# Masks on GpSimd, a later maximum, and gathers that add into the shared output

## The chip, the core and the metric

The program runs on one core of a Trainium2 chip. Its time is device microseconds, the median of three runs: 634.32 us for the kernel before (633.57 to 634.75). The five engines each work through their own queue in program order and wait for each other by semaphores: TensorE (PE; its weight loads are PEld), VectorE (DVE), ScalarE (ACT), GpSimd (POOL) and SyncE (SP), which issues most DMAs.

## The reference

`x` is 8 x 512 x 256 in f32. It is normalised, and goes two ways, a local attention of 32 heads and a mixture of 8 experts with top-1 routing, and the two results are multiplied:

```
xn = layernorm(x)
qkv = xn @ qkv_w.T                       # 32 heads of 8
attn = (q @ k.T) * 8**-0.5
attn = where(m != 0, attn * m, -inf)     # m: local window, keys i-8 .. i+7, weights that fall off
s = softmax(attn) @ v @ proj_w.T + proj_b
out = sum over experts e of where(expert_idx == e, (silu(xs @ gate_w[e]) * (xs @ up_w[e])) @ down_w[e], 0)
shared = silu(xn @ shared_gate_w) * (xn @ shared_up_w) @ shared_down_w
g = silu(out + shared)
x = x + s * g
```

## The kernel before, in words

The attention runs in 64 steps (U). A step n has 64 queries (two blocks of 32) against 47 keys each (KW), for all 32 heads: the scores fill 128 partitions x 16 groups x 47 = 752 elements. The work for a step is spread over three steps of the loop, and each engine has a loop of its own over n = 0 .. 66, written out by hand:

- TensorE, `scores(n)`: for each of the two halves of the heads a bf16 matmul with the identity brings the mask (0 or -3e38) into PSUM (L916), and two f32 matmuls add q times k (L920). It waits until the step before has been read (`a_mul`).
- VectorE, `weigh(n)` (L722): scores times the window's weights, from PSUM into `Sx`. `largest(n)` (L729): the maximum of each row, right behind it.
- GpSimd, `subtract(n)` (L427): `Sx` minus the maximum, in place.
- ScalarE, `exps(n-1)` (L500): exp, first in the step after.
- VectorE, `flipped(n-1)` (L751): two transposes into `PTs`, in the step after, behind `largest(n)`.
- TensorE, `weighted(n-2)` (L945): times v. VectorE, `invert(n-2)` (L759): reciprocals of the sums. ScalarE, `o_out(n-2)` (L470): four copies PSUM to `Or`. VectorE, `divide(n-2)` (L768) and `turned(n-2)` (L776): normalise, transpose into `OT`. TensorE then projects (`output`, L953) and VectorE adds the bias (`attention`, L794), each second step.

Beside that run the routing (steps 8 to 10, with scatters from GpSimd up to step 16), the shared expert of a batch in steps n % 8 = 0 .. 5 (gates sg at 0 and 2, su at 1 and 3, sd at 4 and 5, which ScalarE copies into the shared rows and posts with `f_sh`), the projections of q and k0 at n % 4 = 0 and of k1 at n % 4 = 1 (ScalarE copies them, `qk_out`, behind its `silu` in the step), and from step E0 = 18 to step 39 the 39 expert tiles, two a step.

The final part handles 16 pairs c of token tiles. `silu_at` puts pair c into step 41 + c for c up to 13, pairs 14 and 15 into steps 61 and 62; `result_at` is one step later, or more. `gather(c)` fetches the experts' rows of the pair into a buffer `Y` by two indirect DMAs (L439), for c = 0 .. 2 in step 40, then for pair c + 3 in the step after silu's issue point for c. `combine(c)` on GpSimd adds `Y` to the shared rows (L447). ScalarE's `silu(c)` takes the tanh of the sum into `Y` (L554), VectorE's `silu(c)` multiplies (L800), and `result(c)` does the product with the attention (L807) and the sum with x (L810), which SyncE stores.

Of the kernel before, what the change touches and what calls it, by code (L numbers as in the profile page):

```python
# [11 lines left out]
ALU = mybir.AluOpType  # L12
# [3 lines left out]
P = 128  # L16
BATCH, SEQ, C = 8, 512, 256
# [4 lines left out]
KC = C // P  # L22
# [6 lines left out]
QB = 32  # L29
# [34 lines left out]
C_M = C_ID + P  # L64
C_BIAS = C_M + KW
C_HEAD = C_BIAS + C
C_STAY = C_HEAD + HS
C_TRI, C_ONE = C_STAY, C_STAY + P
C_FIRST = C_ONE + P
C_TILE = C_FIRST + E  # L70
# [4 lines left out]
def constants(bias):  # L75

    c = np.zeros((P, C_END), np.float32)
    c[:, C_ID:C_ID + P] = np.eye(P)
    c[:, C_BIAS:C_BIAS + C] = bias
    c[:, C_HEAD:C_HEAD + HS] = np.arange(P)[:, None] // HD % HS == np.arange(HS)  # L80
    c[:, C_TRI:C_TRI + P] = np.triu(np.ones((P, P)), 1)
    c[:, C_ONE:C_ONE + P] = 1.0
    c[:, C_FIRST:C_FIRST + E] = E - np.arange(E)
    c[:, C_TILE:C_TILE + NT] = np.arange(NT)
    at = np.arange(KW)[None, :] - (np.arange(P) % QB)[:, None]
    band = (at >= 0) & (at < 2 * WIN)
    d = np.abs(at - WIN).astype(np.float32)
    c[:, C_M:C_M + KW] = np.where(band, (WIN - d / 2.0) / WIN * np.float32(HD ** -0.5), 1.0)
    key = np.arange(KW)[None, :]
    kinds = (band & (key >= WIN), band, band, band, band, band & (key < QB + WIN))  # L90
    c[:, C_MASK:] = np.concatenate([np.where(k, 0.0, NEG) for k in kinds], 1)
    return c


# [3 lines left out]

def mask_kind(n):
    return 0 if n % UB == 0 else 2 if n % UB == UB - 1 else 1  # L100


def first_key(n):
# [48 lines left out]
def build(nc, x, wqkv_d, wproj_d, router_w, gate_w, up_w, down_w, sgate_w, sup_w, sdown_w,  # L152
# [3 lines left out]
    with ctx:  # L156
# [3 lines left out]
        def sem(name):  # L160
            return ctx.enter_context(nc.semaphore(name))
# [52 lines left out]
        XR = [EB[:, (3 + i) * CT * C:(4 + i) * CT * C] for i in range(3)]  # L214

        ident = cst[:, C_ID:C_ID + P]
        mw = cst[:, C_M:C_M + KW]
        bias = cst[:, C_BIAS:C_BIAS + C]
        tri = rcst[:, C_TRI - C_STAY:C_TRI - C_STAY + P]
# [7 lines left out]
        def shared_rows(t):  # L227
# [10 lines left out]
            sem("r_" + n) for n in ("sc", "tanh", "sce", "oh", "cnt", "slot", "row", "tab"))  # L238
        r_scat = [sem(f"r_scat{i}") for i in range(SENDS)]
        m_full = [sem(f"m_full{i}") for i in range(MB)]  # L240
        a_qk, a_S, a_mul, a_max, a_sub, a_exp, a_PT, a_V, a_PV, a_O, a_rec, a_nrm, a_OT, a_s = (
            sem("a_" + n) for n in ("qk", "S", "mul", "max", "sub", "exp", "PT", "V", "PV", "O", "rec", "nrm", "OT", "s"))
        x_v, x_vd = ([sem(f"x_{n}{i}") for i in range(2)] for n in ("v", "vd"))
        f_tg, f_ag, f_hT, f_sh = (sem("f_" + n) for n in ("tg", "ag", "hT", "sh"))
        b_in, b_wd, b_st = ([sem(f"b_{n}{i}") for i in range(k)] for n, k in (("in", 4), ("wd", 2), ("st", 3)))
        b_wg = [sem(f"b_wg{i}") for i in range(2)]
        b_xT, b_et, b_ea, b_hT, b_y = (sem("b_" + n) for n in ("xT", "et", "ea", "hT", "y"))
        d_y, d_x, d_st = ([sem(f"d_{n}{i}") for i in range(3)] for n in ("y", "x", "st"))
        d_z, d_t, d_w, d_g, d_o = (sem("d_" + n) for n in ("z", "t", "w", "g", "o"))

        x_tiles = x.rearrange("(t p) c -> p t c", p=P)
        out_v = out.rearrange("(t p) c -> p t c", p=P)
# [150 lines left out]
        def _(pool):  # L403
# [15 lines left out]
            def scatter(t):  # L419
                pool.wait_ge(r_row, t + 1)  # L420
                pool.indirect_dma_start(xs_dram, bass.IndirectOffsetOnAxis(ap=slot[:, t:t + 1], axis=0),
                                        X[:, t, :], None).then_inc(r_scat[t // (T // SENDS)], 16)

            def subtract(n):
                pool.wait_ge(a_max, n + 1)
                s = Sx[n % 3][:, :, 0:KW]
                nc.gpsimd.tensor_tensor(s, s, mx[n % 3][:, :].unsqueeze(2).broadcast_to([P, 2 * G, KW]),  # L427
                                        ALU.subtract).then_inc(a_sub, 1)

            def gather(c):  # L430
                b = c % 3
                if c == 0:
                    for k in range(3):
                        pool.wait_ge(b_st[k], 16 * len(range(k, NX, 3)))
                if c >= 3:
                    pool.wait_ge(d_w, c - 2)
                for k in range(CT):
                    t = c * CT + k
                    pool.indirect_dma_start(Y[b][:, k * C:(k + 1) * C], None, ys_dram,  # L439
                                            bass.IndirectOffsetOnAxis(ap=slot[:, t:t + 1], axis=0)).then_inc(d_y[b], 16)  # L440

            def combine(c):
                b = c % 3
                z = shared_rows(c * CT).rearrange("p t c -> p (t c)")
                pool.wait_ge(d_y[b], 16 * CT * (c // 3 + 1))
                pool.wait_ge(f_sh, c + 1)
                nc.gpsimd.tensor_tensor(z, Y[b], z, ALU.add).then_inc(d_z, 1)  # L447

            for n in range(LAST + 1):
                for c in silu_at(n):  # L450
                    combine(c)
                if n < U:
                    subtract(n)
                if n == SENT:
                    pool.wait_ge(s_fill, 16 * 10)
                    pool.wait_ge(r_slot, 1)
                for t in range((n - SENT) * SPS, min((n - SENT + 1) * SPS, T)):
                    if t >= 0:
                        scatter(t)
                if n == C_STEP:  # L460
                    for c in range(3):
                        gather(c)
                for c in silu_at(n - 1):
                    if c + 3 < NC:
                        gather(c + 3)

        @block.scalar
        def _(act):
# [80 lines left out]
                act.dma_start(ys_dram[i * P:(i + 1) * P, :], yb[:, i % 3, :]).then_inc(b_st[i % 3], 16)  # L549

            def silu(c):
                act.wait_ge(d_z, c + 1)
                z = shared_rows(c * CT).rearrange("p t c -> p (t c)")
                nc.scalar.activation(Y[c % 3], z, ACT.Tanh, scale=0.5).then_inc(d_t, 1)  # L554

# [60 lines left out]
        def _(dve):  # L616
# [106 lines left out]
                   mw.unsqueeze(1).unsqueeze(1).broadcast_to([P, 2, G, KW]), ALU.mult).then_inc(a_mul, 1)  # L723

            def largest(n):
                dve.wait_ge(a_mul, n + 1)
                if n >= 3:
                    dve.wait_ge(a_sub, n - 2)
                reduce(mx[n % 3][:, :], Sx[n % 3][:, :, 0:KW], AX, ALU.max).then_inc(a_max, 1)  # L729
# [94 lines left out]
            for n in range(LAST + 1):  # L824
                if n < U:
                    weigh(n)
                    largest(n)
                if n == 0:
                    variance(1)
                    deviation(1)  # L830
# [9 lines left out]
                    table()  # L840
                if 0 <= n - 1 < U:
                    flipped(n - 1)
                for i in pair_at(n, 1)[:1]:
                    gate(i)
                    gated(i)
# [8 lines left out]
                if 0 <= n - 2 < U:  # L854
                    divide(n - 2)
                    turned(n - 2)
                for c in silu_at(n):
                    silu(c)
                if n < BATCH:
# [10 lines left out]
        def _(pe):  # L870
# [34 lines left out]

            def scores(n):
                h, u = divmod(n, UH)
                if n == 0:
                    pe.wait_ge(s_cast, 2)
                if n >= 1:  # L910
                    pe.wait_ge(a_mul, n)
                if u == 0:
                    pe.wait_ge(a_qk, 3 * h + 3)
                kind = 2 * mask_kind(n)
                for j in range(KC):
                    mm(psS[:, j, 0:BW], identb[:, :], maskb[:, kind:kind + 2, :, :].rearrange("p i r k -> p (i r k)"),  # L916
                       start=True, stop=False)
                    for i in range(2):
                        k = block_of(n, i) % (HALF // QB)
                        last = mm(psS[:, j, i * HS * KW:(i + 1) * HS * KW], qBD[h % 2][:, j, k, :, :].rearrange("p s q -> p (s q)"),  # L920
                                  kBD[h % 2][:, j, :, k * QB:k * QB + KW], start=False, stop=i == 1)
                last.then_inc(a_S, 1)

            def values(t):
# [160 lines left out]
```

## Time and profile before

| | |
|---|---|
| median of 3 runs | 634.32 us |
| profiled execution | 633.25 us |
| its span in the profile | 631.4 us |
| PE busy | 557.1 us (88%) |
| DVE busy | 403.7 us (64%) |
| ACT busy | 307.9 us (49%) |
| POOL busy | 187.0 us (30%) |
| rate of all DMAs in the first of 40 slices | 292 GB/s |

The span is the profiled execution from its first to its last instruction; the rest of its time lies outside. Busy shares are means over stages with different limits, so they say little of one edit. The stages are told apart by the windows below, and a single step is read in the timeline: an instruction's start, its length, and in brackets how long its engine was idle before it and who ended that.

### The profile page before, as it was taken

What the parts mean: (1) busy time and instruction counts of PE and PEld (TensorE: products, weight loads), DVE (VectorE), ACT (ScalarE), POOL (GpSimd) and SP (SyncE); (2) the same over time, 40 slices, a digit from 0 to 9 for tenths busy, and PEclk for the clock granted to TensorE, in tenths of its full rate; (3) what the DMA queues carried; (4) which work ended last, traced back from release to release, by engine and by line L of the source; (5) the groups of instructions that cost most, each with busy time, mean ns of one, the idle gap of its engine ahead of it and who ended that gap; (6) DMA issues with size and microseconds to landing.
All of it is one profiled execution on the core that took longest, in us unless ns stands there. A gap on an engine that the chain in (4) does not pass through costs nothing. (4 is left out here: it accounts for less than half of the span.)

```text
span 631.4 us, 10599 instructions
## 1 busy us (share of the span) xinstructions
PE 557.1 (88%) x3358; PEld 479.0 (76%) x3358; DVE 403.7 (64%) x853; ACT 307.9 (49%) x762; POOL 187.0 (30%) x160
## 2 busy tenths in 40 slices
PE   1979999979889999999999999999886877769865
PEld 1757898758768999888999888898675655657754
DVE  6766556885756446456446456446688888886873
ACT  1473654458673644533634533645454533636331
POOL 6001011148861111000111000114655545532230
PEclk9989999979999999999999999999989899999997
DMA  8525441113327576576577566443133333331110
GB/s 292 180 70 174 151 141 55 49 49 99 113 92 216 163 223 202 167 203 199 143 218 208 168 203 190 126 129 115 50 110 110 108 99 101 117 102 26 35 42 17
DMA packets 107371, 82.89 MB, mean 131 GB/s; under 512 B 42293, under 2 KB 104757, under 8 KB 107317
## 3 DMA queue, kind: packets, MB, share of 16 engines
q1 hardware_dynamic: 98628, 68.72, 36.9%
q0 software_dynamic: 3072, 8.39, 4.2%
q10 hardware_dynamic: 5616, 5.11, 2.3%
q8 instruction: 27, 0.44, 0.3%
q14 instruction: 28, 0.22, 0.1%
HBM read 59.12 MB, written 23.07 MB: 130 GB/s over the span
## 5 line engine op out<-in xcount | busy, mean ns | idle before, releaser
L427 POOL TENSOR_TENSOR Sx<-Sx,mx 128x752 f32<-128x752 f32 x64 | 93.7, 1465 | 407.1 <-DVE mx L729 406.5
L945 PE MATMUL psV<-VB,PTs 128*128 128x132 f32 x1024 | 133.1, 282 | 30.2 <-ACT Or L470 29.7
L945 PEld LDWEIGHTS psV<-VB,PTs 128*128 128x128 f32 x1024 | 127.1, 193 | 36.1 <-issue 34.9
L470 ACT ACTIVATE Or<-psV 32x128 f32<-32x128 f32 x256 | 68.5, 268 | 150.5 <-DVE rs L759 146.2
L920 PE MATMUL psS<-kBD,qBD 128*128 128x188 f32 x512 | 104.0, 327 | 0.0
L920 PEld LDWEIGHTS psS<-kBD,qBD 128*128 128x128 f32 x512 | 86.9, 193 | 10.4 <-issue 2.2
L751 DVE STREAM_TRANSPOSE PTs<-Sx 128x512 f32<-128x512 f32 x128 | 82.9, 685 | 1.0 <-ACT Sx L500 1.0
L995 PE MATMUL psM<-xT,EB 128*128 128x128 f32 x624 | 76.4, 276 | 0.0
L995 PEld LDWEIGHTS psM<-xT,EB 128*128 128x128 f32 x624 | 73.8, 192 | 2.1 <-ACT qBD L489 1.3
L722 DVE TENSOR_TENSOR Sx<-psS,cst 128x752 f32<-128x752 f32 x64 | 59.6, 932 | 24.5 <-PE psS L920 24.5
L736 DVE SCALAR_TENSOR_TENSOR ea<-et,psM 128x256 f32<-128x256 f32 x39 | 16.4, 421 | 76.3 <-PE psM L995 47.2
L972 PE MATMUL psM<-xnT,wsgu 128*128 128x512 f32 x128 | 61.6, 604 | 2.1 <-DVE ag L783 2.1
L729 DVE TENSOR_REDUCE mx<-Sx 128x16 f32<-128x752 f32 x64 | 59.9, 936 | 2.2
L916 PE MATMUL psS<-maskb,identb 128*128 128x376 bf16 x128 | 41.7, 325 | 17.2 <-DVE Sx L722 16.9
L470 ACT ACTIVATE kBD<-psM 32x272 f32<-32x272 f32 x128 | 49.2, 385 | 14.7 <-PE psM L902 13.6
L500 ACT ACTIVATE Sx<-Sx 128x752 f32<-128x752 f32 x64 | 53.0, 828 | 4.9 <-POOL Sx L427 4.4
L489 ACT ACTIVATE qBD<-psM,cst 128x512 f32<-128x512 f32 x64 | 38.7, 687 | 21.3 <-PE psM L897 21.2
L768 DVE TENSOR_TENSOR O<-Or,rs 128x128 f32<-128x128 f32 x64 | 23.5, 368 | 39.9 <-issue 39.4
L1004 PE MATMUL psM<-EB,ehT 128*128 128x256 f32 x156 | 36.9, 379 | 0.0
L953 PE MATMUL psM<-wp,OT 128*128 128x256 f32 x128 | 33.6, 386 | 3.7 <-DVE OT L776 2.3
L972 PEld LDWEIGHTS psM<-xnT,wsgu 128*128 128x128 f32 x128 | 22.3, 192 | 18.1 <-issue 15.8
L902 PE MATMUL psM<-xnT,wqkv 128*128 128x272 f32 x128 | 34.8, 396 | 0.0
(107 smaller groups left out, 689.3 us busy)
## 6 DMA issues: line engine op xcount, KB each, us to landing
EB<-in_L_ffn_gate_w SPq DMA_DIRECT2D x39, 256.0 KB, 2.9
EB<-in_L_ffn_up_w SPq DMA_DIRECT2D x39, 256.0 KB, 3.6
EB<-in_L_ffn_down_w SPq DMA_DIRECT2D x39, 256.0 KB, 3.1
VB<-v_dram SPq DMA_DIRECT2D x256, 32.0 KB
stage<-xs_dram SPq DMA_DIRECT2D x39, 128.0 KB, 2.2
ys_dram<-yb ACTq DMA_DIRECT2D x39, 128.0 KB, 3.1
xs_dram<-blank SPq DMA_DIRECT2D x9, 512.0 KB, 3.8
v_dram<-vS SPq DMA_DIRECT2D x8, 512.0 KB, 2.9
```

The costliest lines, as they stand in the source:

```text
L427: nc.gpsimd.tensor_tensor(s, s, mx[n % 3][:, :].unsqueeze(2).broadcast_to([P, 2 * G, KW]), ALU.subtract).then_inc(a_sub, 1)
L470: return nc.scalar.activation(dst, src, ACT.Copy)
L489: last = nc.scalar.activation(qBD[h % 2][:, :, :, i, :], q, ACT.Copy, scale=cst[:, C_HEAD + i:C_HEAD + i + 1])
L500: nc.scalar.activation(s, s, ACT.Exp).then_inc(a_exp, 1)
L722: tt(s, psS[:, :, 0:BW].rearrange("p j (g k) -> p j g k", k=KW), mw.unsqueeze(1).unsqueeze(1).broadcast_to([P, 2, G, KW]), ALU.mult).then_ ...
L729: reduce(mx[n % 3][:, :], Sx[n % 3][:, :, 0:KW], AX, ALU.max).then_inc(a_max, 1)
L751: last = nc.vector.transpose(PTs[n % 2][:, k, :, :, :].rearrange("p j i (r q) -> p (j i r) q", q=QB), Sx[n % 3][:, :, k * QB:(k + 1) * QB])
L916: mm(psS[:, j, 0:BW], identb[:, :], maskb[:, kind:kind + 2, :, :].rearrange("p i r k -> p (i r k)"), start=True, stop=False)
L920: last = mm(psS[:, j, i * HS * KW:(i + 1) * HS * KW], qBD[h % 2][:, j, k, :, :].rearrange("p s q -> p (s q)"), kBD[h % 2][:, j, :, k * QB: ...
L945: last = mm(psV[:, j, at:at + HS * VW], PTs[n % 2][:, k, j, i, :], VB[n % 2][:, i, k, :, VW * j:VW * j + VW], start=k == 0, stop=k == 1)
L972: last = mm(ps[:, :], wsgu[:, kc, at:at + P], xnT[:, b, kc, WIN:WIN + SEQ], start=kc == 0, stop=kc == KC - 1)
L995: last = mm(ps[:, f * P:(f + 1) * P], egu[:, i % 2, kc, f * P:(f + 1) * P], xT[:, i % 2, kc, :], start=kc == 0, stop=kc == KC - 1)
```

## The change

Three things change.

1. In steps 0 to 7 and from 18 on (`masked_late`) TensorE issues no mask matmuls. GpSimd adds the mask in `banded(n)`, from a table in f32 in the constants, to what `weigh(n)` wrote. In steps 8 to 17 all stays as it was.
2. In those steps VectorE's `largest(n)` waits for the addition (`a_add`). It stands behind `flipped(n-1)` in steps 0 to 7 and 18 to 37, and behind `turned(n-2)` from step 38 (E0 + NP) on.
3. `gather(c)` adds its rows straight into the shared rows (`compute_op=ALU.add`) and `combine` is gone. The gather for the pair whose tanh is in step n+1 is issued in step n, behind `subtract(n)`, once the shared rows are there (`f_sh`). ScalarE's `silu(c)` waits for the DMA itself (`d_y`).

```diff
+def masked_late(n):
+    return n < BATCH or n >= E0

+            def banded(n):
+                pool.wait_ge(a_mul, n + 1)
+                s = Sx[n % 3][:, :, :].rearrange("p (m r) k -> p m r k", r=HS)[:, :, :, 0:KW]
+                kind = 2 * KC * mask_kind(n)
+                nc.gpsimd.tensor_tensor(s, s, band[:, kind:kind + 2 * KC, :].unsqueeze(2).broadcast_to([P, 2 * KC, HS, KW]),
+                                        ALU.add).then_inc(a_add, 1)
...
             def gather(c):
-                b = c % 3
                 if c == 0:
                     for k in range(3):
                         pool.wait_ge(b_st[k], 16 * len(range(k, NX, 3)))
-                if c >= 3:
-                    pool.wait_ge(d_w, c - 2)
+                pool.wait_ge(f_sh, c + 1)
                 for k in range(CT):
                     t = c * CT + k
-                    pool.indirect_dma_start(Y[b][:, k * C:(k + 1) * C], None, ys_dram,
-                                            bass.IndirectOffsetOnAxis(ap=slot[:, t:t + 1], axis=0)).then_inc(d_y[b], 16)
-
-            def combine(c):
-                b = c % 3
-                z = shared_rows(c * CT).rearrange("p t c -> p (t c)")
-                pool.wait_ge(d_y[b], 16 * CT * (c // 3 + 1))
-                pool.wait_ge(f_sh, c + 1)
-                nc.gpsimd.tensor_tensor(z, Y[b], z, ALU.add).then_inc(d_z, 1)
+                    pool.indirect_dma_start(shared_rows(c * CT)[:, k, :], None, ys_dram,
+                                            bass.IndirectOffsetOnAxis(ap=slot[:, t:t + 1], axis=0),
+                                            compute_op=ALU.add).then_inc(d_y[c % 3], 16)
 
             for n in range(LAST + 1):
-                for c in silu_at(n):
-                    combine(c)
                 if n < U:
+                    if masked_late(n):
+                        banded(n)
                     subtract(n)
...
-                if n == C_STEP:
-                    for c in range(3):
-                        gather(c)
-                for c in silu_at(n - 1):
-                    if c + 3 < NC:
-                        gather(c + 3)
+                for c in silu_at(n + 1):
+                    gather(c)
...
             def silu(c):
-                act.wait_ge(d_z, c + 1)
+                act.wait_ge(d_y[c % 3], 16 * CT * (c // 3 + 1))
+                if c >= 3:
+                    act.wait_ge(d_w, c - 2)
...
             for n in range(LAST + 1):
                 if n < U:
                     weigh(n)
-                    largest(n)
+                    if not masked_late(n):
+                        largest(n)
...
                 if 0 <= n - 1 < U:
                     flipped(n - 1)
+                if n < U and masked_late(n) and n < E0 + NP:
+                    largest(n)
...
                 if 0 <= n - 2 < U:
                     divide(n - 2)
                     turned(n - 2)
+                if E0 + NP <= n < U:
+                    largest(n)
...
                 for j in range(KC):
-                    mm(psS[:, j, 0:BW], identb[:, :], maskb[:, kind:kind + 2, :, :].rearrange("p i r k -> p (i r k)"),
-                       start=True, stop=False)
+                    if not late:
+                        mm(psS[:, j, 0:BW], identb[:, :], maskb[:, kind:kind + 2, :, :].rearrange("p i r k -> p (i r k)"),
+                           start=True, stop=False)
```

VectorE in a step of the final part (step 45), before; `Sx` holds the scores, `mx` the maxima, `PTs` their transposes, `O` and `OT` the output, `xnT` the shared rows, `EB` the buffers of the final part:

```order
L722 TENSOR_TENSOR Sx<-psS,cst 128x16x47
L729 TENSOR_REDUCE mx<-Sx 128x16
L751 STREAM_TRANSPOSE PTs<-Sx 128x512 x2
L759 RECIPROCAL rs<-psV 128x8 x2
L768 TENSOR_TENSOR O<-Or,rs 128x128
L776 STREAM_TRANSPOSE OT<-O 128x4x32
L800 SCALAR_TENSOR_TENSOR xnT<-EB,xnT 128x512
L807 SCALAR_TENSOR_TENSOR X<-xnT,X 128x512
L810 TENSOR_TENSOR EB<-X,EB 128x512
```

The same step on VectorE now:

```order
L726 TENSOR_TENSOR Sx<-psS,cst 128x16x47
L758 STREAM_TRANSPOSE PTs<-Sx 128x512 x2
L766 RECIPROCAL rs<-psV 128x8 x2
L775 TENSOR_TENSOR O<-Or,rs 128x128
L783 STREAM_TRANSPOSE OT<-O 128x4x32
L736 TENSOR_REDUCE mx<-Sx 128x16
L807 SCALAR_TENSOR_TENSOR xnT<-EB,xnT 128x512
L814 SCALAR_TENSOR_TENSOR X<-xnT,X 128x512
L817 TENSOR_TENSOR EB<-X,EB 128x512
```

The maximum has moved from the second place to the place behind the turned output, ahead of the silu.

GpSimd before, from the addition for pair 3 through steps 44 and 45 (gathers of pairs 5 and 6):

```order
L447 TENSOR_TENSOR xnT<-EB,xnT 128x512 [waits f_sh,d_y0]
L427 TENSOR_TENSOR Sx<-Sx,mx 128x16x47 [waits a_max]
L439 DMA EB<-ys_dram,slot 128x256 [waits d_w]
L439 DMA EB<-ys_dram,slot 128x256
L447 TENSOR_TENSOR xnT<-EB,xnT 128x512 [waits f_sh,d_y1]
L427 TENSOR_TENSOR Sx<-Sx,mx 128x16x47 [waits a_max]
L439 DMA EB<-ys_dram,slot 128x256 [waits d_w]
L439 DMA EB<-ys_dram,slot 128x256
```

GpSimd now, steps 44 and 45 (gathers of pairs 4 and 5):

```order
L435 TENSOR_TENSOR Sx<-Sx,cst 128x16x47 [waits a_mul]
L441 TENSOR_TENSOR Sx<-Sx,mx 128x16x47 [waits a_max]
L451 DMA xnT<-ys_dram,slot 128x256 [waits f_sh]
L451 DMA xnT<-ys_dram,slot 128x256
L435 TENSOR_TENSOR Sx<-Sx,cst 128x16x47 [waits a_mul]
L441 TENSOR_TENSOR Sx<-Sx,mx 128x16x47 [waits a_max]
L451 DMA xnT<-ys_dram,slot 128x256 [waits f_sh]
L451 DMA xnT<-ys_dram,slot 128x256
```

The addition of the pair has left the queue, the mask's addition has come in ahead of the subtraction, and the gathers of a step are those that the next step's tanh waits for.

ScalarE now, step 45 (k1 is copied in this step); before, the rows stood in the same order, and the tanh waited for `d_z`:

```order
L502 ACTIVATE Sx<-Sx 128x16x47 [waits a_sub]
L558 ACTIVATE EB<-xnT 128x512 [waits d_w,d_y1]
L472 ACTIVATE kBD<-psM 32x272 [waits a_S,m_full0]
L472 ACTIVATE kBD<-psM 32x272 x3
L472 ACTIVATE Or<-psV 32x128 [waits a_nrm,a_rec]
L472 ACTIVATE Or<-psV 32x128 x3
L472 ACTIVATE xnT<-psM 128x512 [waits m_full1]
```

The copies of k and then those of `Or` stand behind the tanh.

## Rows read from the trace of the kernel before

**Rows 1.** Windows by stage: PE, PEld, DVE, ACT, POOL busy us; PEclk, DMA, GB/s

```profile
27.50:111.60 84.10, 78.44 (x423) 64.88 (x423) 54.51 (x116) 43.68 (x104) 12.19 (x8) 0.98 0.37 122
...
188.20:407.00 218.80, 218.49 (x1473) 196.62 (x1472) 113.47 (x245) 103.29 (x270) 27.52 (x19) 1.00 0.64 190
...
432.00:570.00 138.00, 108.88 (x606) 89.03 (x605) 110.58 (x191) 67.72 (x158) 73.09 (x63) 0.98 0.36 102
```

**Rows 2.** Timeline of light step 55: start us, length us, engine, line, operation

```profile
561.47 0.93 DVE L722 TENSOR_TENSOR Sx<-psS,cst 128x752 f32<-128x752 f32 x1
...
562.44 0.94 DVE L729 TENSOR_REDUCE mx<-Sx 128x16 f32<-128x752 f32 x1
...
563.29 1.29 DVE L751 STREAM_TRANSPOSE PTs<-Sx 128x512 f32<-128x512 f32 x2
...
563.46 1.45 POOL L427 TENSOR_TENSOR Sx<-Sx,mx 128x752 f32<-128x752 f32 x1 [3.75 <-DVE mx L729]
...
564.78 1.11 ACT L470 ACTIVATE Or<-psV 32x128 f32<-32x128 f32 x4 [5.61 <-DVE rs L759]
...
565.98 0.29 DVE L768 TENSOR_TENSOR O<-Or,rs 128x128 f32<-128x128 f32 x1 [1.23 <-issue]
...
566.54 0.90 DVE L722 TENSOR_TENSOR Sx<-psS,cst 128x752 f32<-128x752 f32 x1
```

**Rows 3.** Timeline of VectorE: the weighing of steps 39, 47, 48, 49 and 63

```profile
427.14 0.94 DVE L722 TENSOR_TENSOR Sx<-psS,cst 128x752 f32<-128x752 f32 x1
...
492.25 0.94 DVE L722 TENSOR_TENSOR Sx<-psS,cst 128x752 f32<-128x752 f32 x1
...
500.62 0.93 DVE L722 TENSOR_TENSOR Sx<-psS,cst 128x752 f32<-128x752 f32 x1
...
510.51 0.93 DVE L722 TENSOR_TENSOR Sx<-psS,cst 128x752 f32<-128x752 f32 x1
...
611.33 0.93 DVE L722 TENSOR_TENSOR Sx<-psS,cst 128x752 f32<-128x752 f32 x1
```

**Rows 4.** Timeline near the end: the exp of step 63 and its flip

```profile
615.78 0.83 ACT L500 ACTIVATE Sx<-Sx 128x752 f32<-128x752 f32 x1
...
616.64 1.30 DVE L751 STREAM_TRANSPOSE PTs<-Sx 128x512 f32<-128x512 f32 x2 [0.16 <-ACT Sx L500]
```

**Rows 5.** Timeline of TensorE: a mask matmul and its follower

```profile
563.26 0.32 PE L916 MATMUL psS<-maskb,identb 128*128 128x376 bf16 x1
...
563.42 0.80 PE L920 MATMUL psS<-kBD,qBD 128*128 128x188 f32 x4
```

**Rows 6.** Timeline of VectorE and GpSimd at the silu of pair 14

```profile
603.20 0.65 DVE L800 SCALAR_TENSOR_TENSOR xnT<-EB,xnT 128x512 f32<-128x512 f32 x1
603.31 1.68 POOL L447 TENSOR_TENSOR xnT<-EB,xnT 128x512 f32<-128x512 f32 x1 [1.75 <-ACT xnT L470]
```

**Rows 7.** Timeline of ScalarE: copies of q and k0 (step 40)

```profile
433.16 2.42 ACT L489 ACTIVATE qBD<-psM,cst 128x512 f32<-128x512 f32 x4 [0.74 <-PE psM L897]
...
435.46 1.57 ACT L470 ACTIVATE kBD<-psM 32x272 f32<-32x272 f32 x4
```

**Rows 8.** Timeline of GpSimd: the last two gathers, each for one tile

```profile
557.48 0.97 POOL L439 DMA_INDIRECT EB<-ys_dram,slot  x1
558.76 0.95 POOL L439 DMA_INDIRECT EB<-ys_dram,slot  x1 [0.32 <-issue]
```

**Rows 9.** Windows, POOL alone: a stretch in which only the gather moves data

```profile
560.40:561.20 0.80, 0.00 (x0) 1.00 0.59 164
```

**Rows 10.** Timeline of step 45: result's product, GpSimd's addition, tanh

```profile
481.15 2.01 DVE L807 SCALAR_TENSOR_TENSOR X<-xnT,X 128x512 f32<-128x512 f32 x1
481.32 1.28 POOL L447 TENSOR_TENSOR xnT<-EB,xnT 128x512 f32<-128x512 f32 x1
482.63 0.63 ACT L554 ACTIVATE EB<-xnT 128x512 f32<-128x512 f32 x1 [1.36 <-POOL xnT L447]
```

**Rows 11.** Groups by line: busy us, mean ns, idle before, of result's product

```profile
L807 DVE SCALAR_TENSOR_TENSOR X<-xnT,X 128x512 f32<-128x512 f32 x14 | 19.0, 1360 | 0.1
```

More of the change, by code:

```diff
@@ L66 @@
 C_HEAD = C_BIAS + C
-C_STAY = C_HEAD + HS
+C_BAND = C_HEAD + HS
+C_STAY = C_BAND + 12 * KW
 C_TRI, C_ONE = C_STAY, C_STAY + P
@@ L91, in constants @@
     c[:, C_MASK:] = np.concatenate([np.where(k, 0.0, NEG) for k in kinds], 1)
+    c[:, C_BAND:C_STAY] = np.tile(c[:, C_MASK:].reshape(P, 3, 1, 2 * KW), (1, 1, KC, 1)).reshape(P, 12 * KW)
     return c
@@ L216, in build @@
         ident = cst[:, C_ID:C_ID + P]
+        band = cst[:, C_BAND:C_BAND + 12 * KW].rearrange("p (m k) -> p m k", k=KW)
         mw = cst[:, C_M:C_M + KW]
@@ L240, in build @@
         m_full = [sem(f"m_full{i}") for i in range(MB)]
-        a_qk, a_S, a_mul, a_max, a_sub, a_exp, a_PT, a_V, a_PV, a_O, a_rec, a_nrm, a_OT, a_s = (
-            sem("a_" + n) for n in ("qk", "S", "mul", "max", "sub", "exp", "PT", "V", "PV", "O", "rec", "nrm", "OT", "s"))
+        a_qk, a_S, a_mul, a_add, a_max, a_sub, a_exp, a_PT, a_V, a_PV, a_O, a_rec, a_nrm, a_OT, a_s = (
+            sem("a_" + n) for n in ("qk", "S", "mul", "add", "max", "sub", "exp", "PT", "V", "PV", "O", "rec", "nrm", "OT", "s"))
         x_v, x_vd = ([sem(f"x_{n}{i}") for i in range(2)] for n in ("v", "vd"))
@@ L248, in build @@
         d_y, d_x, d_st = ([sem(f"d_{n}{i}") for i in range(3)] for n in ("y", "x", "st"))
-        d_z, d_t, d_w, d_g, d_o = (sem("d_" + n) for n in ("z", "t", "w", "g", "o"))
+        d_t, d_w, d_g, d_o = (sem("d_" + n) for n in ("t", "w", "g", "o"))
         x_tiles = x.rearrange("(t p) c -> p t c", p=P)
@@ L725, in largest @@
             def largest(n):
-                dve.wait_ge(a_mul, n + 1)
+                if masked_late(n):
+                    dve.wait_ge(a_add, len([k for k in range(n + 1) if masked_late(k)]))
+                else:
+                    dve.wait_ge(a_mul, n + 1)
                 if n >= 3:
@@ L907, in scores @@
                 h, u = divmod(n, UH)
-                if n == 0:
+                late = masked_late(n)
+                if n == BATCH:
                     pe.wait_ge(s_cast, 2)
@@ L920, in scores @@
                         last = mm(psS[:, j, i * HS * KW:(i + 1) * HS * KW], qBD[h % 2][:, j, k, :, :].rearrange("p s q -> p (s q)"),
-                                  kBD[h % 2][:, j, :, k * QB:k * QB + KW], start=False, stop=i == 1)
+                                  kBD[h % 2][:, j, :, k * QB:k * QB + KW], start=late, stop=late or i == 1)
                 last.then_inc(a_S, 1)
```

## The prediction

> **What bounds the kernel now.** I read the busy time by stage first, then the timeline of single steps, then the waits. One step handles 64 queries of all heads; W(n) is the moment VectorE starts to weigh the scores of step n, M(n) the end of its maximum. Three stages matter. In steps 0 to 7 and above all 18 to 37 (the stage with the experts) TensorE is full: 218.49 of 218.80 us, in steps 0 to 7 78.44 of 84.10 [rows 1]. From step 39 on it has slack (108.88 of 138.00), and VectorE is at 110.58 of 138.00 [rows 1]. The steps there show no slack on VectorE's own chain. A light step lasts 566.54 - 561.47 = 5.07 us and is this chain: weigh, maximum, transposes (flip), reciprocals, ScalarE's four copies Or, product O, turned output, next weigh [rows 2]. A step with the final part (silu, result) lasts 500.62 - 492.25 = 8.37, and with a shared gate (sg) in it 510.51 - 500.62 = 9.89, so 1.5 more: ScalarE's tanh and VectorE's product stand between Or and O [rows 3].
>
> In before, the softmax of a step has nearly a step to spare: the maximum of step n ends right behind W(n), GpSimd's subtraction takes 1.45, ScalarE's exp 0.83 [rows 2, 4], and only the flip in step n+1 wants the result. The gathers have more than a step to spare as well, since they are issued two or three steps ahead.
>
> **Part 1, the mask matmuls.** Each starts 0.16 us before its follower [rows 5] (the 0.32 beside it overlaps). Two a step, in 54 of 64 steps: 17.3 us of TensorE's stream. It is worth its price only where TensorE is the bound: 20 steps x 0.32 = 6.4, and of the 8 early steps (2.6) some 1.6, since TensorE waits there now and then. **-8.0**. In the late stage it is worth nothing: VectorE's chain covers it.
>
> **Part 2, the mask on GpSimd.** No such addition is in the trace. The subtraction of the same 752 elements takes 1.45 [rows 2], the addition of 512 elements with both inputs dense 1.28 [rows 6], so 1.9 for 752. The bounds are 1.45 and 1.9. In steps below 38 the maximum stands behind the flip, which ends 1.2 us after it starts, so VectorE waits 0.3 to 0.8 us and the gate of an expert comes up that much later; the trace has about that much idle there before the gate. Hidden, **0**. From 38 on it ends long before the maximum. Beside the addition VectorE does flip and reciprocals, each with one input at most in SBUF. Loading the wider constants (564 columns more, 289 KB) delays the start by about 1 us at the 292 GB/s of the first slice; in step 0 the maximum (0.94) no longer stands ahead of the variance, which ScalarE's next work waits for: **0**.
>
> **Part 3, the maximum behind the turned output (steps 38 to 63).** The number of instructions on VectorE's chain is the same, but now M(n) lies right before W(n+1), and the flip of step n+1 needs this step's subtraction and exp. The loop from M to M: handover and subtraction 0.08 + 1.45, exp with handovers 0.9, so the flip starts at M + 2.4; flip to Or 1.49, Or to O 1.20, O to the next instruction 0.56, maximum 0.94 [rows 2, 4]. Sum 6.6, against 5.07. The wait is 1.45 in a light step. On ScalarE the copies of q and k stand between exp and Or: 433.16 to 437.03, 3.9 for q and k0 (n divisible by 4), 1.6 for k1 (the step after) [rows 7]. So:
> Step 39: 6.6. Step 40 (q, k0, sg): 2.4 + 3.9 + 1.2 + 1.5 + 0.56 + 0.94 = 10.5. Step 56 the same. Step 57: 2.4 + 1.6 + 1.2 + 1.5 (product, turned, maximum) = 6.7. Step 58: 6.6 + 1.5 = 8.1. Step 60: 6.6.
> Where VectorE has the result's two products behind the maximum (steps after 54, 58 and 62), its own work is the longer way: the product ends 0.56 behind the subtraction that holds it up [rows 10], at M + 2.1 (2.5 where a silu comes first, Part 4), the sum takes 0.7, weighing 1.0, flip to maximum 4.2. That gives 8.0 (59) and 8.4 (55, 63).
>
> **Part 4, the gathers.** Before, the gather of pair c+3 was issued in the step of pair c, GpSimd added it, and ScalarE's tanh found it ready. Now the gather for step n+1 stands behind step n's subtraction, which stands behind M(n), and the tanh of step n+1 waits for its landing. Behind the tanh on ScalarE wait the copies of q and k, and Or; for Or wait O, the turned output and M(n+1). That closes a second loop, once a step: 0.08 + 1.45, then 0.4 (VectorE's silu has both inputs in SBUF and was at work 0.11 before the GpSimd addition which took 1.68 in place of 1.28 [rows 6]), 0.14 to the gather, 3.65 from the first issue to the last byte (557.48, the second at 558.76, bytes until about 561.15 [rows 8, 9]), tanh 0.6 [rows 10], Or to O 1.20, 0.56, 0.94: 9.0, and 8.6 where no silu precedes. Add what the trace has no row for: the last byte to the waiting engine, and the cost of adding on the way. Call it a. The nearest row is the gather itself, a = 0; the upper end is twice the work on GpSimd (2.2) and twice the burst of data (0.8 us [rows 9]), 3.0. I take 0.8, the burst once more. (The Trainium skill, "DMA: Bandwidth & Descriptors", Rules for kernel authors, says that an accumulating DMA reads its destination and writes it later. No run shows it yet; it speaks for a burst twice as long rather than for 0.)
> What goes: GpSimd's additions. They held up the result's product, 2.01, where the silu of the same size takes 0.65 [rows 6, 10]. But the subtraction now lies at just that place, right behind the maximum and beside silu and result. VectorE's own way stays at 8.4 to 8.6, and the gather's loop is above it.
> Steps 41 to 54: 8.6 + 1.6 (k1) = 10.2 for 41; 13 x 9.0 = 117.0; q and k0 in 44, 48, 52 and k1 in 45, 49, 53: 16.5; sg in 42, 48, 50: 4.5. Sum 148.2 + 14a. In before they are 14 x 8.37 + 3 x 1.5 = 121.7 [rows 3]. Steps 61 and 62: 8.6 + 9.0 + 2a.
>
> **The sum.** M(38) comes where W(39) was, less part 1, with 0.3 for the wait: 427.14 - 8.0 + 0.3 = 419.4 [rows 3]. Steps 39 and 40: 17.1. Steps 41 to 54: 148.2. Step 55: 8.4. Steps 56 to 60: 10.5 + 6.7 + 8.1 + 8.0 + 6.6 = 39.9. Steps 61 to 63: 26.0. The tail was 631.4 - 611.33 = 20.1 from W(63) [rows 3]; 1.9 of it lies before M(63), and the chain of step 61 is done by then, some 2.7: 15.5. Together 674.5, with 16a = 12.8: span 687.3. The profiled execution is 1.85 above its span, and the median 1.07 above that execution: **690 us**, 56 slower. By parts: -8 from TensorE, the rest of the way, +64, from the two loops.
>
> **Rivals.**
> (A) The gather isn't waited for: the addition lands early enough or ScalarE's other work covers it, and only the softmax loop costs. Steps 41 to 54 stay at some 123, steps 55 to 63 at 71: 419.4 + 17.1 + 123 + 71 + 15.5 + 2.9 = 649. For it: in before the tanh waits little. Against: from the gather's issue to the tanh ScalarE has only the exp to do, 0.9 of 3.65.
> (B) Faster. Flip and Or do not wait, because VectorE reaches the maximum early: with GpSimd's additions gone, the results' products are back at some 0.65 (mean 1.36 [rows 11], 14 of them, 9.9 us), and -8.0 comes on top: 634.3 - 17.9 = 616. The point that decides is M(n) to M(n+1): below 8.4 in the final steps and below 5.1 in light ones. Against: 2.4 us of subtraction and exp do not fit in the 1.0 that weighing leaves.
> (C) Both loops, and a price above mine. Either a is 2 or more (16 x 1.2 = 19 on top, 709), or the port is held differently. On that, the row first: the result's product is recorded from 481.15, 0.17 before GpSimd's addition, and still ended 0.56 after it [rows 10], so GpSimd got in between. If VectorE kept its place over both products, the subtraction would end 0.9 later in 14 steps: +12, 702. The Trainium skill ("SBUF — State Buffer", Who interferes with whom) has it that whichever of the two starts first keeps the shared pair for its instruction; the 1.68 of rows 6 agrees, the recorded starts of rows 10 do not, unless the product had not really begun.
>
> **How the numbers follow.** Forecast 0.66, A 0.11, B 0.10, C 0.13. The forecast's own range, a from 0 to 2 or so: 677 to 708. The range reaches down to A and up into C: 646 to 712. A difference under 0.2% (1.3 us) can't be told from none. Faster 0.10, same 0.01, slower 0.89.
>
> **What would show it.** Right: in the profile after, ScalarE's tanh (L558) waits 2 us and more for the gathers in steps 41 to 54; steps with q and k0 last about 13.5, those without 9.5 to 10; the flip (L758) waits for exp in light steps, which last 6.6; the expert stage is about 6 us shorter; result's product is still near 2 us in many steps. Wrong: a period of 8.4 in the final steps (A), or light steps of 5.1 (B). The forecast falls if the tanh is found waiting for nothing, or if M(n) isn't followed by the gather on GpSimd.

## The result, and the profile after

The changed kernel takes 718.11 us (715.9 to 719.29, four runs), the kernel before 634.27 in the same comparison: a ratio of 1.1324, 95% interval 1.1299 to 1.1349. It is 84 us slower. The forecast was 690 us, range 646 to 712: the direction and the two loops were right, and the size was not.

The windows by stage of the profile after (columns as in [rows 1]):

```profile
190.00:404.00 214.00, 212.89 (x1440) 193.65 (x1439) 112.82 (x242) 104.28 (x272) 58.37 (x39) 1.00 0.66 192
...
430.00:600.00 170.00, 101.81 (x440) 80.92 (x439) 83.59 (x147) 53.43 (x125) 82.67 (x49) 0.79 0.28 59
600.00:717.00 117.00, 77.65 (x356) 65.81 (x354) 63.52 (x125) 35.76 (x89) 49.13 (x31) 0.76 0.19 42
```

The expert stage is still TensorE's, and a few us shorter. Behind 430 us no engine is busy for more than 60% of the time up to 600: TensorE 101.81 of 170, where [rows 1] has 108.88 of 138. Where no engine is near full, the length of a step is set by who waits for whom. From the waits of the whole execution after (who waited for whom; us in total, times, longest):

```profile
POOL Sx L441 <- DVE mx L736: 205.6, 59, 10.1
...
DVE O L775 <- issue: 104.5, 33, 9.1
ACT Sx L502 <- POOL Sx L441: 94.5, 29, 4.2
...
ACT EB L558 <- DMA xnT<-ys_dram,slot: 81.8, 14, 6.2
```

Two of them are new and are the two loops: exp (L502) waits for the subtraction, 94.5 us against 4.4 before, and the tanh (L558) for the gathers. The product O (L775) follows from them: it stands behind ScalarE's copies `Or`, which stand behind the tanh, though the profile puts its 104.5 us down to "issue". One period of the gather's loop, from the maximum of step 45 to that of step 46, in the timeline after (the rows that answer to [rows 8, 10]):

```profile
502.11 0.89 DVE L736 TENSOR_REDUCE mx<-Sx 128x16 f32<-128x752 f32 x1
502.93 0.68 DVE L807 SCALAR_TENSOR_TENSOR xnT<-EB,xnT 128x512 f32<-128x512 f32 x1
503.09 1.82 POOL L441 TENSOR_TENSOR Sx<-Sx,mx 128x752 f32<-128x752 f32 x1 [6.70 <-DVE mx L736]
503.52 1.94 DVE L814 SCALAR_TENSOR_TENSOR X<-xnT,X 128x512 f32<-128x512 f32 x1
...
505.06 1.82 POOL L451 DMA_INDIRECT xnT<-ys_dram,slot  x1 [0.15 <-issue]
...
507.19 1.55 POOL L451 DMA_INDIRECT xnT<-ys_dram,slot  x1 [0.30 <-issue]
...
511.73 0.63 ACT L558 ACTIVATE EB<-xnT 128x512 f32<-128x512 f32 x1 [5.96 <-DMA xnT<-ys_dram,slot]
512.27 1.09 ACT L472 ACTIVATE Or<-psV 32x128 f32<-32x128 f32 x4
513.45 0.29 DVE L775 TENSOR_TENSOR O<-Or,rs 128x128 f32<-128x128 f32 x1 [4.96 <-issue]
...
514.08 0.89 DVE L736 TENSOR_REDUCE mx<-Sx 128x16 f32<-128x752 f32 x1
```

Read it in order: maximum until 503.00, subtraction from 503.09, first gather 505.06, second 507.19, tanh 511.73, Or, O, next maximum until 514.97: 11.97 us, against 8.37 before. From the first issue to the tanh it is 6.67 us, where the forecast had 3.65 + 0.8 = 4.45. The subtraction takes 1.82 beside VectorE's silu and 1.45 in the light step below (the forecast had 1.45 + 0.4; this delay by an operation of the other engine is called the lock from here on), and result's product is held up to 1.94, just as GpSimd's addition had done it in [rows 10].

A light step after (step 57; answers to [rows 2]):

```profile
643.05 1.45 POOL L441 TENSOR_TENSOR Sx<-Sx,mx 128x752 f32<-128x752 f32 x1 [7.19 <-DVE mx L736]
...
644.53 0.83 ACT L502 ACTIVATE Sx<-Sx 128x752 f32<-128x752 f32 x1 [3.78 <-POOL Sx L441]
...
645.39 1.31 DVE L758 STREAM_TRANSPOSE PTs<-Sx 128x512 f32<-128x512 f32 x2 [1.25 <-ACT Sx L502]
...
648.65 0.89 DVE L736 TENSOR_REDUCE mx<-Sx 128x16 f32<-128x752 f32 x1
```

The flip waits 1.25 us for exp, and from maximum to maximum it is 6.58 (642.96 to 649.54), where 6.7 was forecast.

### The profile page after: what moved, and what is told of

It is laid out like the page before. It is cut to its first block and busy times, and to the rows that moved or that the text cites. A ratio compares the mean times of both kernels' runs of the same rounds, so it can differ in the third digit from the quotient of the medians.

```text
span 717.5 us, 10418 instructions
## 1 busy us (share of the span) xinstructions
PE 580.2 (81%) x3250; PEld 498.4 (69%) x3250; DVE 401.9 (56%) x853; ACT 308.2 (43%) x762; POOL 283.8 (40%) x198
## 3 DMA queue, kind: packets, MB, share of 16 engines
q0 software_dynamic: 6144, 8.39, 6.1%
## 5 line engine op out<-in xcount | busy, mean ns | idle before, releaser
L959 PE MATMUL psV<-VB,PTs 128*128 128x132 f32 x1024 | 157.9, 316 | 76.8 <-ACT Or L472 76.8
L959 PEld LDWEIGHTS psV<-VB,PTs 128*128 128x128 f32 x1024 | 149.1, 224 | 86.8 <-issue 86.2
L441 POOL TENSOR_TENSOR Sx<-Sx,mx 128x752 f32<-128x752 f32 x64 | 99.1, 1549 | 205.7 <-DVE mx L736 205.6
L435 POOL TENSOR_TENSOR Sx<-Sx,cst 128x752 f32<-128x752 f32 x54 | 99.3, 1838 | 196.7 <-DVE Sx L726 196.7
L934 PE MATMUL psS<-kBD,qBD 128*128 128x188 f32 x512 | 97.3, 331 | 15.0 <-DVE Sx L726 14.8
L502 ACT ACTIVATE Sx<-Sx 128x752 f32<-128x752 f32 x64 | 53.2, 831 | 94.6 <-POOL Sx L441 94.5
L775 DVE TENSOR_TENSOR O<-Or,rs 128x128 f32<-128x128 f32 x64 | 18.5, 288 | 105.0 <-issue 104.5
L736 DVE TENSOR_REDUCE mx<-Sx 128x16 f32<-128x752 f32 x64 | 58.5, 914 | 12.1 <-POOL Sx L435 11.8
L914 PE MATMUL psM<-xnT,wqkv 128*128 128x272 f32 x128 | 39.1, 434 | 18.7 <-ACT qBD L491 18.6
L451 POOL DMA_INDIRECT xnT<-ys_dram,slot x28 | 46.6, 1665 | 6.4 <-issue 5.9
L558 ACT ACTIVATE EB<-xnT 128x512 f32<-128x512 f32 x14 | 8.8, 629 | 81.8 <-DMA xnT<-ys_dram,slot 81.8
L914 PEld LDWEIGHTS psM<-xnT,wqkv 128*128 128x128 f32 x128 | 26.0, 210 | 24.6 <-ACT qBD L491 20.1
```

The source lines that it names most:

```text
L435: nc.gpsimd.tensor_tensor(s, s, band[:, kind:kind + 2 * KC, :].unsqueeze(2).broadcast_to([P, 2 * KC, HS, KW]), ALU.add).then_inc(a_add, 1)
L502: nc.scalar.activation(s, s, ACT.Exp).then_inc(a_exp, 1)
L914: last = mm(ps[:, 0:KH], wqkv[:, kc, C + j * P:C + (j + 1) * P], xnT[:, b, kc, at:at + KH], start=kc == 0, stop=kc == KC - 1)
L959: last = mm(psV[:, j, at:at + HS * VW], PTs[n % 2][:, k, j, i, :], VB[n % 2][:, i, k, :, VW * j:VW * j + VW], start=k == 0, stop=k == 1)
```

## The experiments

All ratios are to runs of the kernel before on the same chip. "Final steps" are those with silu and result; steps whose shared gate or whose copies of q and k make them longer are named apart. M(n) and W(n) are as in the prediction. The diffs are shortened: "..." and comments in them are not in the kernels, and declarations are left out.

### e1: the old gathers in the changed kernel

```diff
-                for c in silu_at(n + 1):
-                    gather(c)
+                if n == C_STEP: ... gather(0), gather(1), gather(2)
+                for c in silu_at(n - 1): ... gather(c + 3)      # into Y; combine(c) adds on GpSimd, as before
```

> The changed kernel with the gathers, their issue points and GpSimd's addition as they were before; masks on GpSimd and the late maximum stay. Theory T1 (two loops from maximum to maximum, of which the gather's is the dearer): the final steps fall from 12.0 to about 8.4 to 9.7 us, light steps stay at 6.6, ScalarE's tanh waits little; 645 to 662 us. Rival T2 (TensorE at half its clock and the softmax loop explain the time, the tanh's wait is only where it shows): still above 690.

Measured: 674.21 us, ratio 1.0644 (1.0614 to 1.0674). 44 less than the changed kernel, so T2's number fell, but T1's was 12 too low. The timeline of e1, step 47 to 48, shows why:

```profile
512.84 1.24 POOL L453 DMA_INDIRECT EB<-ys_dram,slot  x1 [0.15 <-issue]
...
514.38 0.95 POOL L453 DMA_INDIRECT EB<-ys_dram,slot  x1 [0.30 <-issue]
...
515.35 1.29 POOL L461 TENSOR_TENSOR xnT<-EB,xnT 128x512 f32<-128x512 f32 x1
...
516.67 0.63 ACT L570 ACTIVATE EB<-xnT 128x512 f32<-128x512 f32 x1 [3.11 <-POOL xnT L461]
```

Its data had landed long before, but GpSimd's addition for the next tanh stands in GpSimd's queue behind this step's subtraction and two issues (the next step's tanh is the one at 516.67). With the late maximum the tanh waits for that queue: final steps of 9.1 us, and 13.1 with q and k0. This is the nearest kernel to rival A of the prediction that keeps the buffers, and 25 us above its number (649): A had let the tanh go free because it had been free before, and here it waits for GpSimd's addition.

### e2: the same gathers, without adding

```diff
                     pool.indirect_dma_start(shared_rows(c * CT)[:, k, :], None, ys_dram,
-                                            bass.IndirectOffsetOnAxis(ap=slot[:, t:t + 1], axis=0),
-                                            compute_op=ALU.add).then_inc(d_y[c % 3], 16)
+                                            bass.IndirectOffsetOnAxis(ap=slot[:, t:t + 1], axis=0)).then_inc(d_y[c % 3], 16)
```

> The changed kernel, with gathers at the same place in GpSimd's queue that copy into the shared rows and don't add (the experts' rows replace the shared expert's). T1 with the addition as the price that was mis-sized (a = 3.0, of which the plain gather has 0.3): GpSimd's issue falls from 1.6 to 1.8 to about 1.0 us each, first issue to tanh from 6.7 to 4.0, final steps from 12.0 to 9.3; 16 x 2.7 = 43 less, 675 us (668 to 683). Rival T3 (a is the price of waiting for any gather, of the completion or of HBM behind the expert's store, not of adding): 710 or more.

This kernel leaves the addition out.

Measured: 688.72 us, ratio 1.0864 (1.084 to 1.0888). 29.4 less than with the addition, over 16 pairs 1.8 each; a plain final step takes 9.95 to 10.0 in place of 12.0. From its timeline:

```profile
505.44 1.24 POOL L451 DMA_INDIRECT xnT<-ys_dram,slot  x1 [0.15 <-issue]
...
506.99 0.95 POOL L451 DMA_INDIRECT xnT<-ys_dram,slot  x1 [0.30 <-issue]
...
510.03 0.63 ACT L557 ACTIVATE EB<-xnT 128x512 f32<-128x512 f32 x1 [3.88 <-DMA xnT<-ys_dram,slot]
```

First issue to tanh 4.59, of which 1.55 to the second issue and 3.04 from there to the tanh. Adding makes the two pieces 2.13 and 4.54. So of the 3.0 us of "a" in such a step 2.1 go with the addition (0.6 for GpSimd's longer issues, 1.5 for the way from the second issue to the tanh), and 0.9 a plain gather has as well.

About half of that 0.9 is no price of the gather. In 12 of the 16 pairs, here and in the changed kernel, the first issue runs beside VectorE's result, and there it is longer: 1.24 us against 0.97 plain (in e1 too, where no tanh waits for it), 1.82 against 1.55 adding. The other four pairs (0, 1, 14, 15) show the gather by itself. First issue to tanh is 4.0, 4.1, 4.5 and 4.0 us plain, and 5.6, 5.8, 5.6 and 5.6 adding. For pair 15 the windows (as in [rows 9]) show the bytes of the second gather, about 131 KB each time; first before, then the issue, the burst and the tanh in the changed kernel:

```profile
560.40:561.00 0.60, 0.00 (x0) 1.00 0.78 219
...
686.23 1.55 POOL L451 DMA_INDIRECT xnT<-ys_dram,slot  x1 [0.30 <-issue]
...
688.40:689.60 1.20, 1.05 (x1) 1.00 0.82 109
...
689.95 0.63 ACT L558 ACTIVATE EB<-xnT 128x512 f32<-128x512 f32 x1 [4.86 <-DMA xnT<-ys_dram,slot]
```

The burst begins 1.6 us behind the start of its issue before (558.76) and 2.2 now, which is the longer issue, and lasts 1.2 us in place of 0.6. The tanh follows some 0.4 behind it (in e2, pair 15, 0.5). These windows can be read to 0.2 us. So in a quiet stretch, with nothing beside the gather, adding costs two issues longer by some 0.55 each and a burst longer by 0.6; with 0.4 for the completion that is some 2 us over the way to the last byte before, and a plain gather has about 0.5 of it. Both theories were off in the time: most of the cost is the addition, and the rest is in part the completion, in part what goes on beside the gather.

### e3: each gather one step earlier where it can be

```diff
-                for c in silu_at(n + 1):
-                    gather(c)
+                for c in range(NC):
+                    if n == gather_at(c):    # silu's step - 2, or - 1 where f_sh comes only then
+                        gather(c)
```

> The changed kernel, with each gather issued one step earlier where the shared rows are already there (pairs 1 to 11), the rest in place. T1: the loop through the gather is open in steps 42 to 52, the tanh finds its data, these steps take what VectorE needs, 8.4 to 8.8 (10 with q and k0), about 3.3 less each: 718 - 11 x 3.3 = 682 us (670 to 690). T2: no change from 718.

Measured: 669.93 us, ratio 1.0566 (1.0543 to 1.059), 48 less than the changed kernel for a move of two rows in a queue. The final steps whose gather was moved take 8.7 us where neither a gate nor copies of q and k0 stand in them: 496.36 - 487.55 = 8.81 and 505.09 - 496.36 = 8.73 between the weighings. The tanh runs as soon as exp is done:

```profile
495.13 0.83 ACT L509 ACTIVATE Sx<-Sx 128x752 f32<-128x752 f32 x1 [4.12 <-POOL Sx L447]
...
495.86 0.61 ACT L565 ACTIVATE EB<-xnT 128x512 f32<-128x512 f32 x1
```

T2 falls, and T1 holds in kind: 682 was 12 too high, at the lower end of its range, for it left out that steps with copies gain more (step 48: 11.2 in place of 17.4). Steps 53, 54, 61 and 62, whose gathers stayed, are as long as in the changed kernel to within 0.5 us.

### e4: the maximum behind the flip in the late steps as well

```diff
-                if n < U and masked_late(n) and n < E0 + NP:
+                if n < U and masked_late(n):
                     largest(n)
...
-                if E0 + NP <= n < U:
-                    largest(n)
```

> The changed kernel, with the maximum behind the flip in the late steps too, as in steps 18 to 37. T1: exp is off the chain, light steps last 5.1 to 5.5 instead of 6.6; the loop through the gather now takes two steps (17.4 us plus ScalarE's copies), so final steps last 8.7 to 10: 645 us (638 to 660). A rival (the gather's wait costs the same wherever the maximum stands, since the tanh still waits for it): only the light steps gain, 700 to 708.

Measured: 644.0 us, ratio 1.0157 (1.0135 to 1.0179): T1's number within 1. The tanh still waits for the gathers, 54.2 us between 430 and 560, and the steps are short nonetheless, 9.4 on average from M(40) to M(54) in place of 13.4 (8.0 to 8.3 for six of the 14, 12.0 to 13.2 from M(44), M(48) and M(52), behind which the copies of q and k0 come), and 5.6 for light ones. The wait in the row costs its length only if the next maximum stands behind it.

### e5: the late maximum alone

```diff
                 if n < U:
                     weigh(n)
-                    largest(n)
+                    if n < E0 + NP:
+                        largest(n)
...
                     turned(n - 2)
+                if E0 + NP <= n < U:
+                    largest(n)
```

> The kernel before, with one edit: from step 38 on VectorE's maximum stands behind the turned output. Masks and gathers as before. T1 (the loops from maximum to maximum): as in e1, whose late steps have the same two loops, 6.6 us in light steps and 9.1 in final ones (subtraction, two gathers, GpSimd's addition, tanh), but without the 8 us that TensorE saves: 682 us (676 to 688). Rival T4 (part of e1's time is GpSimd's load with the mask's additions): 650 to 670.

Measured: 684.96 us, ratio 1.0792 (1.077 to 1.0815). Moving one instruction per step costs 51 us. Its late steps are e1's to 0.04 us (light 6.57, final 9.1), so with the late maximum the mask's additions cost nothing there, and the mask matmuls that TensorE is spared gain nothing; T4 falls.

### e6: masks on GpSimd below step 38 alone

```diff
 def masked_late(n):
-    return n < BATCH or n >= E0
+    return n < BATCH or E0 <= n < E0 + NP
```

(Old gathers; no maximum behind the turned output.)

> The kernel before, with the masks on GpSimd and the maximum behind the flip in steps 0 to 7 and 18 to 37 alone; later steps and gathers as before. T1: TensorE's stream is 0.32 us shorter in 28 steps, of which the 20 with experts count in full: 626 us (624 to 629).

Measured: 624.98 us, ratio 0.9867 (0.9836 to 0.9898). This is the part of the change that pays: 8.2 us by the spans (623.2), all of it before step 39 (W(39) at 418.50 against 427.14 in [rows 3]), and the later steps are as they were.

### e8: e6, with adding gathers issued early

Edits of e6 and of e3 together, without the buffers.

> As e6, and in place of the buffers and GpSimd's addition the adding gathers, issued a step earlier where the shared rows are there. T1: with the maximum right behind the weighing no lock meets the result's product (0.69 in place of 2.0), VectorE's chain in a final step falls from 8.4 to 7.1, and the gathers have over a step to land: 626 - 16 = 610 us (603 to 618). Rival T5 (GpSimd's longer issues of 1.6 to 1.8 us hold up its subtraction, and so exp and flip): 622 or more.

Measured: 617.58 us, ratio 0.9734 (0.9715 to 0.9753). Final steps last 7.04 (7.44 with a projection). The groups by line of e8 show what went, against 1360 in [rows 11]:

```profile
L821 DVE SCALAR_TENSOR_TENSOR X<-xnT,X 128x512 f32<-128x512 f32 x14 | 9.6, 683 | 0.1
```

Result's product is free of the lock, 0.68. The gain stopped 7 us short of T1's number, inside its range, in steps 53, 54, 61 and 62 (10.02, 9.15, 8.10 and 10.50), whose shared rows come only one step ahead.

### e9: the gathers alone

The kernel before with the new `gather`, its issue point, and the tanh's wait; no `combine`.

> The kernel before, with the gathers of the changed kernel alone: adding, issued behind the subtraction of the step ahead of the tanh, no addition on GpSimd. Masks and maximum as before. T1: the tanh waits for the landing, but the maximum of the next step does not stand behind it, so the loop spans two steps: 7.1 to 7.5 us a final step plus what ScalarE's copies add, 633 us (627 to 640). Rival (the wait of the tanh costs its whole length every step): above 660.

Measured: 639.02 us, ratio 1.0066 (1.0043 to 1.0089), 4.7 us slower. Final steps last 7.0 to 7.4 without a gate or copies, and 11.1 to 12.4 where ScalarE copies q and k0: the loop over two steps, as T1 had it, and inside its range, with the copies dearer than I took them.

### e10: e8, the last four pairs in buffers

```diff
+BUFFERED = 12
...
+                for c in silu_at(n):
+                    if c >= BUFFERED:
+                        combine(c)
...
+                for c in silu_at(n - 1):
+                    if c + 3 >= BUFFERED and c + 3 < NC:
+                        fetch(c + 3)
```

> As e8, with pairs 12 to 15 handled as before the change (buffers, fetched two to three steps ahead, GpSimd's addition), because their shared rows are there only one step ahead and steps 53, 54, 61 and 62 lasted 10.0, 9.1, 8.1 and 10.5 us in e8. T1 (the tanh of these pairs waits for an adding gather): these steps fall to 8.4, 7.6, 5.8 and 7.6, 609 us (606 to 613). Rival (their length is that of ScalarE's copies and the shared expert's): 616 to 619.

Measured: 610.3 us (609.51 to 612.2), ratio 0.9631 (0.9613 to 0.9649). Steps 53, 54, 61 and 62 last 8.37, 7.56, 5.65 and 7.56. It is the fastest of all here, 24 us under the kernel before.

### e11: e8 with late masks on GpSimd

```diff
-    return n < BATCH or E0 <= n < E0 + NP
+    return n < BATCH or n >= E0
```

(The maximum behind the flip throughout.)

> As e8, but with the masks on GpSimd in the late steps too and the maximum behind the flip there. T1: the maximum waits 0.4 us for the mask in each of 26 late steps, TensorE's saving is worth nothing there, and the subtraction comes later: 632 us (626 to 640). Rival (late masks pay once the gathers are out of the way): below 617.

Measured: 636.99 us, ratio 1.0041 (1.0026 to 1.0057), 19 more than e8. Light steps last 5.60 in place of 5.04, plain final ones 8.0 to 8.1 in place of 7.0 to 7.4.

### e12: TensorE kept busier

```diff
                 for j in range(KC):
+                    for _ in range(10 if n >= E0 + NP else 0):
+                        mm(psS[:, j, 0:BW], identb[:, :], maskb[...], start=True, stop=True)
```

> The changed kernel, with 20 more bf16 matmuls (identity times mask) at the head of the scores of each late step, 3.2 us of stream, whose result the scores overwrite; they stand in the gap in which TensorE waited. T1 (the clock of 0.79 and 0.76 lies off the chain): the granted clock of the late steps rises, the steps keep their length, 718 us (716 to 721). Rival T2 (the low clock is a cause): clearly below 710.

Measured: 729.69 us, ratio 1.152 (1.1488 to 1.1552). The windows of e12:

```profile
430.00:600.00 170.00, 137.22 (x724) 100.19 (x722) 83.72 (x146) 53.88 (x123) 83.75 (x50) 0.92 0.29 64
600.00:700.00 100.00, 86.87 (x515) 66.72 (x515) 53.13 (x101) 31.40 (x76) 45.54 (x28) 0.97 0.19 43
```

T2 falls, and T1's number was missed by 12 us. The granted clock rose from 0.79 to 0.92 (430 to 600), and from 0.76 to 0.97 (from 600 on). Between the maxima of steps 42 and 54 nothing moved: 163.69 us in the changed kernel, 163.94 in e12. Of the two levels, 1.2 and 2.4 GHz, TensorE's is the lower for part of that stage in the changed kernel (windows of 0.25 us in step 45 read 0.50 at 505.75 and 1.00 at 506.25), and between steps 42 and 54 that costs nothing. Outside them the clock's share isn't told apart from that of the added stream, which has no room there: M(42) comes 4.0 us later than in the changed kernel, and steps 55 to 60 take 5.6 us more (step 60: 7.48 against 6.65).

## Why the prediction was wrong, point by point

The prediction's own list, in ends of maxima, forecast with a = 0.8 against measured:

| stretch | forecast | measured |
|---|---|---|
| M(38) | 419.4 | 419.52 |
| steps 39 and 40 | 17.1 | 16.83 |
| steps 41 to 54 | 148.2 + 11.2 | 188.20 |
| steps 55 to 60 | 48.3 | 47.30 |
| steps 61 to 63 | 26.0 + 1.6 | 29.49 |
| tail | 15.5 | 16.16 |
| span | 687.3 | 717.5 |

- **Part 1, right.** W(39) came 7.4 us earlier in the changed kernel and 8.6 in e6; the forecast was 8.0. The masks from step 38 on were worth nothing: the late steps of e5, in which TensorE issues them, and of e1, in which it does not, are equal to 0.04 us.
- **Part 2, right below step 38.** The addition takes 1.66 us with nothing beside it, between the bounds of 1.45 and 1.9. It held the maximum up by 0.6 us at most (11.8 us in 21 waits), and with it W(39) was 0.6 from the forecast, so it cost next to nothing there. In late steps with the early maximum it does cost (e11); the forecast did not need that case.
- **Part 3, right.** Light steps 6.6, steps with q, k0 and sg 10.25 against 10.5, steps 57 to 60 within 0.25 of the forecast.
- **Part 4, the step that failed.** The loop, its members and its order were right. The term "a" was mis-sized: I took 0.8, "the burst once more", and it is 2.9 on average in steps 41 to 54 (188.2 less 148.2, over 14) and 1.9 in steps 61 and 62. In sum that is 28.8 and 1.9 us; all other terms together miss by 0.5 the other way, and the span by 30.2. In a quiet stretch a is about 2 (e2, pair 15): two longer issues, 1.1 in all, a burst longer by 0.6 and 0.4 for the completion, less 0.15 since the last byte before came at 561.0 and not at 561.15. So "the burst once more" was nearly the burst's part, and the issues and the completion were put at nothing. In steps 43 to 54 some 1 us comes on top with result and the other transfers beside the gather. I had both ends, 0 and 3.0, and chose near the lower end because its row was the nearest. But that row was of an operation nobody waited for: it ended at the last byte, and stood where no result runs beside the issue. The choice by nearness was the mistake, and my own range of a, "0 to 2 or so", left out the end I had worked out. That the upper end met the 3.0 of a final step is partly luck: it had the issues twice as long (2.2) and nothing for the completion or for what runs beside.
- **Where 16 x a comes from.** The error was multiplied by 16 since the term stands in a loop. A range for a term of a loop is as wide as the term's times the turns: with a up to its own end of 3.0 the range would have reached 725, and mine ended at 712.
- **Rival A**'s condition, a gather nobody waits for, is met in steps 43 to 52 of e3: 9.3 us a step on average, where A had 123 / 14 = 8.8. **Rival B**'s gain is there, but in another kernel: e8 and e10 have both its terms, the 8 us and the product without the lock.
- **Rival C**'s first branch is what happened, at a chance of 0.13: a is above 2. Its 709 was 9 short, for a is 3 in most steps. Its second branch, the port held for both products, fell. The rows came out as the forecast had them: subtraction 1.82 beside silu, and result's product still held up by it, 1.94. They fit a subtraction that got the port between the two products of VectorE, and then the recorded start of an instruction that is queued behind another isn't when it takes the port. The Trainium skill ("SBUF — State Buffer", Who interferes with whom) has it that whoever issues first gets the shared pair for the whole instruction. The trace agrees in that the hold ended with the instruction: the subtraction was held up by 0.37 (1.82 against 1.45) by one product and not by both.

By parts, as the experiments bear it out: on the way from the kernel before over e5 and e1 to the changed kernel the ratio goes 1, 1.0792, 1.0644, 1.1324, so the late maximum costs 50 us, the masks give back 9, and the gathers cost 43. Each alone, they are 51 more (e5), 9 less (e6) and 5 more (e9), which makes some 46 and not 84: the late maximum closes a loop over one step that the early one leaves open over two.

**Left open.** The way from the second issue to the tanh is 4.2 to 4.8 us for the pairs 2 to 13 and 3.7 to 3.9 for the pairs 0, 1, 14 and 15, in whose steps no result runs beside the issue; plain, it is 3.0 to 3.3 against 2.7 to 3.2. The windows of step 45 point to the other DMAs: from 510.50 to 511.75 they read 234 to 325 GB/s where the adding gather alone has 109, but no run takes away only those or only VectorE's part.

## What to carry to other kernels

In a software pipeline written by hand, ask of each moved instruction which instruction of the next step now stands behind it: follow the ring through all engines until it is back, and add it up. A wait costs its length only if its ring is the longest (e4, e9); then everything else on that ring, ScalarE's copies here, is laid bare too. For a transfer that nobody waited for, the trace has no price of waiting: take the end that includes completion, and multiply by the turns.

## What the runs showed of the hardware that I had not expected

- An indirect gather that adds: GpSimd's issue 1.55 us in place of 0.95 (1.82 in place of 1.24 beside VectorE's result), 1.0 to 1.5 us more from the second issue to the waiting engine in most pairs, the burst of 128 KB 1.2 us in place of 0.6, and 6144 packets in the software queue against 3072, for the same 8.39 MB with the scatters, which did not change.
- GpSimd's addition of the 752 elements takes 1.66 behind nothing and 1.67 behind a plain gather (507.95 in e2). Behind an adding one it is recorded with 2.23 (508.18), but from 0.56 before the recorded end of the issue (508.74) until 1.67 behind it: the two records overlap, and the addition costs no more.
- GpSimd's subtraction takes 1.45 where its second operand is one value for each row of 47, and the addition 1.66 for the same 752 elements with a second operand that changes from element to element.
